# Norm sums folded on VectorE ahead of TensorE's products, and the square moved up ScalarE's step

## The reference, cut to what matters

```
for i in range(DEPTH):                                  # 6
    x = attn_layer(shift_tokens(x), ...) + x            # the sum is called x1 in the kernel
    x = ffn_layer(shift_tokens(x), g, bln, W1, b1, W2, b2) + x

def ffn_layer(x, g, bln, W1, b1, W2, b2):
    mu = x.mean(-1, keepdims=True)
    var = ((x - mu) ** 2).mean(-1, keepdims=True)
    xn = (x - mu) / jnp.sqrt(var + 1e-05) * g + bln
    ...
```

## Time and profile before

| | |
|---|---|
| median of 3 runs | 3278.15 us (3271.11 to 3278.32) |
| profiled execution: span from first to last instruction | 3280.4 us |
| its own time beside the span | the page gives none apart from the span, which lies 2.2 us above the median of the runs |
| TensorE matmul busy | 3087.2 us, 94% |
| TensorE weight load busy | 2736.1 us, 83% |
| VectorE busy | 2638.4 us, 80% |
| ScalarE busy | 2534.1 us, 77% |
| GpSimd busy | 2084.0 us, 64% |
| mean granted TensorE clock | 0.963 |

### The profile page before, as it was taken

The page is one execution under the profiler, slowest core; times in us unless marked ns, Lnnn a source line. Parts: engine busy times, 40 slices in busy tenths (PEclk is TensorE's granted clock), DMA queues, the critical chain, the costliest instruction groups (busy, mean ns, idle before and its releaser), DMA issues. The chain is left out here.

```text
span 3280.4 us, 80720 instructions
## 1 busy us (share of the span) xinstructions
PE 3087.2 (94%) x29936; PEld 2736.1 (83%) x29936; DVE 2638.4 (80%) x5117; ACT 2534.1 (77%) x7059; POOL 2084.0 (64%) x1536
## 2 busy tenths in 40 slices
PE   5898886689999999999999999999999999999997
PEld 4666664479998999989999989999899998999996
DVE  3378888878789888788878898878988878888884
ACT  2787885478787888788888888888788887888784
POOL 5347655776666666666666676667676767666661
PEclk8888996799999999999999999999999999999998
DMA  3111100110001000001100011000100000110000
GB/s 128 55 36 49 59 4 7 42 36 11 2 2 34 25 26 2 2 21 33 31 2 2 11 34 39 1 2 2 37 26 22 2 1 21 33 31 7 8 5 26
DMA packets 27780, 75.04 MB, mean 23 GB/s; under 512 B 4120, under 2 KB 9848, under 8 KB 27256
## 3 DMA queue, kind: packets, MB, share of 16 engines
q1 hardware_dynamic: 22224, 52.63, 5.1%
q0 software_dynamic: 4864, 16.78, 1.6%
q10 hardware_dynamic: 304, 0.47, 0.1%
HBM read 65.68 MB, written 4.19 MB: 21 GB/s over the span
## 5 line engine op out<-in xcount | busy, mean ns | idle before, releaser
L1596 POOL TENSOR_TENSOR turned<-by_cos,turned 128x512 f32<-128x512 f32 x384 | 494.5, 1288 | 827.5 <-DVE turned L2101 827.0
L1600 POOL TENSOR_TENSOR rnorm<-norm,half 128x8 f32<-128x8 f32 x384 | 789.1, 2055 | 0.0
L1883 ACT ACTIVATE prob<-ps_s,ebias,rnorm 128x128 f32<-128x128 f32 x1536 | 681.8, 457 | 64.9 <-DVE ebias L2122 64.2
L2115 DVE TENSOR_REDUCE negmax<-ps_s 128x8 f32<-128x1024 f32 x192 | 235.0, 1224 | 284.0 <-PE ps_s L1698 283.9
L1892 ACT ACTIVATE prob_t<-ps_t 128x512 f32<-128x512 f32 x384 | 230.3, 600 | 223.4 <-PE ps_t L1707 218.8
L2130 DVE TENSOR_TENSOR prob<-prob,rinv 128x512 f32<-128x512 f32 x384 | 375.8, 979 | 13.1
L1642 PE MATMUL ps_qk<-w_hi,x_hi 128*128 128x512 f32 x768 | 336.8, 438 | 18.8 <-DVE turned L2101 12.2
L1787 PE MATMUL ps_f<-hid_hi,w_hi 128*128 128x256 f32 (+1 forms) x1056 | 309.3, 293 | 5.7 <-DVE hid_lo L2176 5.6
L1883 ACT ACTIVATION_READ_ACCUMULATOR prob<-ps_s,ebias,rnorm 128x1 f32 x1536 | 311.1, 203 | 0.0
L1642 PE MATMUL ps_qk<-w_lo,x_hi 128*128 128x512 f32 x768 | 305.8, 398 | 0.0
L1642 PE MATMUL ps_qk<-w_hi,x_lo 128*128 128x512 f32 x768 | 305.7, 398 | 0.0
(11 more groups left out here) (289 smaller groups left out, 9779.6 us busy)
## 6 DMA issues: line engine op xcount, KB each, us to landing
w_raw<-in_w_qkv SPq DMA_DIRECT2D x24, 768.0 KB, 4.8
w_raw<-in_w SPq DMA_DIRECT2D x12, 693.0 KB, 4.0
w_raw<-in_w_o SPq DMA_DIRECT2D x12, 512.0 KB, 3.4
w_raw<-in_w SPq DMA_DIRECT2D x6, 768.0 KB, 4.4
x_tok<-in_x SPq DMA_DIRECT2D x8, 256.0 KB, 2.7
kept<-x_t SPq DMA_DIRECT2D x8, 256.0 KB, 2.0
w_raw<-kept SPq DMA_DIRECT2D x8, 256.0 KB, 3.1
out<-rows_out SPq DMA_DIRECT2D x8, 256.0 KB, 2.2
```

Source lines behind the costliest of these rows:

```text
L1596: G.tensor_tensor(turned[:, k, :], by_cos[:, :], turned[:, k, :], ALU.add).then_inc(s["turned"], 1)
L1600: G.tensor_tensor(rnorm[:, i % RR, :], norm2[:, k, :], half[:, :], ALU.pow).then_inc(s["rnorm"], 1)
L1883: last = A.activation(prob[:, k, h, :], half_bank(h % 2, k)[:, T(h // 2)], ACT.Exp, bias=ebias[:, i // NU % 2, k, h:h + 1], scale=rnorm[:, ...
L2115: V.tensor_reduce(negmax[:, k, :, :].rearrange("p u (c o) -> p o u c", o=2), ps_s[:, :, :].rearrange("p o (u c k) -> p o u c k", u=NU, c=2 ...
```

## The change

- `add_x` on VectorE has a second instruction: it waits for the first, and adds the two halves of x1 (in the shifted view) into `halves`, 128x256, which lies in `hidden[:, 2, :]`.
- `mean_mm` is one product (of `halves`) instead of two.
- A new piece `add_squares` on VectorE (offset 18, behind `soften` and ahead of `rotate`) waits for ScalarE's squares and adds their two halves into `squares`, 128x256, which lies in `gate[:, 2, :]`.
- `var_mm` has two products instead of four, and waits for `add_squares`.
- `square` on ScalarE stands ahead of `project` in step 17 instead of behind `flip_prob`. Its waits are the same, its wait for `hid_lo` too.
- The semaphores `lx1` and `cent` become `x1_and_halves` and `cent_and_squares`, which count two steps for each pass.

```diff
+    halves, squares = hidden[:, KT, :], gate[:, KT, :]
...
         def mean_mm(q):
-            E.wait_ge(s["lx1"], q + 1)
+            E.wait_ge(s["x1_and_halves"], 2 * q + 2)
...
-            for kt in range(KT):
-                last = E.matmul(ps_f[1][:, 0:N], mean_w[:, :], shifted(x1[:, q % 2, :])[:, kt, :], start=kt == 0, stop=kt == KT - 1)
-            last.then_inc(s["mean"], 1)
+            E.matmul(ps_f[1][:, 0:N], mean_w[:, :], halves, start=True, stop=True).then_inc(s["mean"], 1)

         def var_mm(q):
-            E.wait_ge(s["cent2"], q + 1)
+            E.wait_ge(s["cent_and_squares"], 2 * q + 2)
             for u in range(NU):
-                for kt in range(KT):
-                    last = E.matmul(ps_f[1][:, N + u:N + u + 1], cent_sq[:, kt, T(u)], mean_w[:, 0:1], start=kt == 0,
-                                    stop=kt == KT - 1)
+                last = E.matmul(ps_f[1][:, N + u:N + u + 1], squares[:, T(u)], mean_w[:, 0:1], start=True, stop=True)
             last.then_inc(s["var"], 1)
...
         def square(q):
-            A.wait_ge(s["cent"], q + 1)
+            A.wait_ge(s["cent_and_squares"], 2 * q + 1)
             if q:
                 A.wait_ge(s["hid_lo"], 2 * q)
...
+            for q in passes(t, 17):
+                square(q)
             for i in units(t, 0):
                 project(i)
...
-            for q in passes(t, 17):
-                square(q)
             for c in lates(t, 13):
                 flip_heads(c)
...
         def add_x(q):
...
-                            ALU.add).then_inc(s["lx1"], 1)
+                            ALU.add).then_inc(s["x1_and_halves"], 1)
+            V.wait_ge(s["x1_and_halves"], 2 * q + 1)
+            if q:
+                V.wait_ge(s["gated"], 2 * q - 1)
+            by_half = shifted(x1[:, q % 2, :])
+            V.tensor_tensor(halves, by_half[:, 0, :], by_half[:, 1, :], ALU.add).then_inc(s["x1_and_halves"], 1)
...
+        def add_squares(q):
+            V.wait_ge(s["cent2"], q + 1)
+            V.tensor_tensor(squares, cent_sq[:, 0, :], cent_sq[:, 1, :], ALU.add).then_inc(s["cent_and_squares"], 1)
...
             for r in groups(t, 4):
                 soften(r)
+            for q in passes(t, 18):
+                add_squares(q)
             for i in units(t, 1):
                 rotate(i)
```

More of the change, by code:

```diff
@@ L1420 @@
     "qk_square v_copied qk_t prob prob_t attn_hi cent2 lin_hi hid_read_act gelu hid_hi "
-    "qk_by_sin norm2 norm2_floor negmax ebias rinv prob_unit attn_lo lx1 cent spread normed lin lin_lo hid_read_dve gated "
+    "qk_by_sin norm2 norm2_floor negmax ebias rinv prob_unit attn_lo x1_and_halves cent_and_squares spread normed lin lin_lo hid_read_dve gated "
     "fed summed rnorm turned k_unit rstd hid_lo lset"
@@ L1793, in w_2_mm @@
                 E.wait_ge(s["low"], OTHER * (q // B + 1))
-            E.wait_ge(s["lx1"], min(q + 2, PASSES))
+            E.wait_ge(s["x1_and_halves"], 2 * min(q + 2, PASSES) - 1)
             for j in range(NJ):
@@ L2152, in center @@
             V.tensor_tensor(cent[:, :, :], shifted(x1[:, q % 2, :]), ps_f[1][:, 0:N].unsqueeze(1).broadcast_to([P, KT, N]),
-                            ALU.subtract).then_inc(s["cent"], 1)
+                            ALU.subtract).then_inc(s["cent_and_squares"], 1)
+        def add_squares(q):
+            V.wait_ge(s["cent2"], q + 1)
+            V.tensor_tensor(squares, cent_sq[:, 0, :], cent_sq[:, 1, :], ALU.add).then_inc(s["cent_and_squares"], 1)
         def take_spread(q):
```

## The result

| | before | after |
|---|---|---|
| median of the runs | 3275.65 us (4 runs, 3271.11 to 3278.32) | 3306.63 us (4 runs, 3304.18 to 3310.97) |
| ratio, 95% interval | | 1.0102 (1.0084 to 1.0119) |
| profiled execution: own time, span | -, 3280.4 us | 3310.97 us, 3309.7 us |
| TensorE busy, mean granted clock | 3087.2 us, 0.963 | 3057.8 us, 0.962 |

The change costs 1.0%, some 31 us. The forecast was 3305 us, with a range of 3290 to 3322, and a rise of 26.8 us. TensorE is busy 29 us less and the span is 29 us longer: the removed products are gone, and more than their time has come back as waiting.

What follows compares the result with a forecast made beforehand. TensorE is busy 94%, but its waits for other engines decide. 10.5 + 7.0 + 4.6 + 5.1 - 0.4 = +26.8 us gives a span of 3307 us, a median of 3305 us, range 3290 to 3322.

Steps and rivals of the forecast that it cites:

- mean_mm, gain 0: TensorE, border of steps 16 and 17: 0.44 us saved is lost in flip_qk's wait for prob_t; gain 0.
- ordinary passes: The 30 passes without weight splits: new stall of 0.75 us less var_mm's 0.40, 0.35 us longer each, +10.5 us.
- var_mm, 0.40: TensorE: four fewer records, no wait right behind, so 0.40 us gained per pass, 18.8 us over 47.
- halves, 0.47: VectorE, second instruction of add_x: pieces behind it 0.47 us later, rotate and GpSimd's chain 0.17 us late.
- kind 22: Passes like 22, five with weight splits, VectorE without a gap: +1.8 us less 0.40, 1.4 each, +7.0 us.
- The square's place, the main term: ScalarE, ahead of project: square's wait for hid_lo holds the queue, making flip_qk of step 18 stall 0.75 us.
- The chain: From the end of hid_lo through square, squares of q and k, copies and prob_t to flip_qk: 2.44 us.
- Weight-split passes: The 15 passes like 22, 23 and 24, in which weights are split: +7.0, +4.6 and +5.1 us.
- kind 23: Passes like 23, five; hid_lo's lateness set by a weight split: +1.3 us less 0.4 each, +4.6 us.
- kind 24: Passes like 24, five with weight splits: flip_qk +1.4 us, less 0.4 each, +5.1 us.
- No third cost there: Later in step 18: ScalarE catches up, rotate 0.5 us later, but GpSimd had waited 2.40 us; no further cost.
- The port of VectorE and GpSimd: Exclusion rule for both new VectorE additions against GpSimd's SBUF reads; left out of the forecast, sum otherwise 3324, chance 0.12.

Runs made afterwards that it cites:

- The mean's half alone: Kernel before with only `halves` added on VectorE and one product in mean_mm; square and var_mm as before: 3278.08 us, ratio 1.0008.
- `prob_t` out of the way: Kernel before with ScalarE's copy prob_t made between v_tok and v_shift in the step of mean_mm: 3266.08 us, ratio 0.9971.
- The loosened wait: Changed kernel, but the square waits only for the first part of hid_lo (2q - 1), not both: 3266.99 us, ratio 0.9976 to the kernel before.
- the move alone: Kernel before with nothing but the square moved ahead of project: 3325.73 us, ratio 1.0157.
- the old place: Changed kernel with the square back behind flip_prob, its wait unchanged: 3287.14 us, ratio 1.0034 to the kernel before.
- a second addition: Changed kernel with the wait for hid_lo loosened to its first part and add_squares done twice: 3288.08 us, ratio 1.0038 to the kernel before.

## Why the prediction was right, point by point

- **mean_mm, gain 0: shown.** The mean's half alone changes ordinary passes by 0.00 to 0.03 us, and with `prob_t` out of the way the same place gives 0.37.
- **var_mm, 0.40: shown.** In step 18, from `flip_qk` to `flip_prob`, the kernel after takes 3.02 us and the kernel before 3.43: 0.41.
- **halves, 0.47 for the pieces behind it, 0.17 through to GpSimd, and 0.47 ahead of kind 22: shown.** L2127 starts 1.27 us behind `add_x` (0.79 before): 0.48. `hid_lo` ends 7.51 us behind the transposes of step 16 instead of 7.36: 0.15. Ahead of kind 22: 0.45.
- **The square's place, the main term: shown.** The loosened wait removes it with everything else in place, and the move alone brings it about. The square's waits in the list are 105.1 us, a little above the 80 to 100 foretold. The chain measures 2.37 us (1806.22 to 1808.59) for 2.44; the link taken at 0.33 was 0.27. With that the stall is 0.65 us instead of 0.75, and an ordinary pass +0.24 instead of +0.35. (The bounds were carried over inexactly: 0.5 and 1.1 us less 0.40 are 0.1 and 0.7, not 0.14 and 0.75. That moves the range by 1 or 2 us.)
- **Weight-split passes: mechanism shown, sizes near.** Kind 22 came out at 1.0 to 1.45 in the pass plus 0.5 ahead of it (1.4 forecast for both), kind 23 at 0.6 to 0.8 (0.95 forecast), kind 24 at 0.9 to 1.2 (1.05).
- **Not forecast: the clock.** Two episodes in passes 6 and 30 cost some 2.8 us each above the others of their kind. Between 5 and 6 of the 31 us are theirs.
- **The total: in part luck.** The rise was forecast at 26.8 us and is 31.0. That 3305 lies within 2 us of 3306.63 comes also from the median before, which a fourth run lowered by 2.5 us. And the terms of the 26.8 missed in both directions: some 2.5 us too much in the ordinary passes, 1 too much in kind 23, 1.6 too little in and ahead of kind 22 even without the clock, and nothing for the clock (5.6 us) and for the end (3.4 us in the profile). The mechanism and the places are right; the closeness of the number is not evidence for it.
- **"No third cost there": right for this kernel only.** The late `rotate` did no harm because TensorE was late too. Where the stall is cured it comes out: the old place gives +0.34% instead of the -0.35% that I had expected, and a second addition is paid in full. The step that failed is the one on what is late next: it weighed `rotate` against GpSimd and its results in step 19, and not against `project` of step 18, which waits for it by `qk_by_sin`. The list of waits before, 1000 to 3200 us, had a row on this very wait, from the passes of kind 22, which the prediction left out:

```profile
PE ps_qk L1642 <- DVE turned L2101: 0.9, 5, 0.2
```

- **The port of VectorE and GpSimd.** The Trainium skill's rule (SBUF — State Buffer, § Who interferes with whom) that two SBUF inputs of a VectorE instruction block GpSimd's reads would have made GpSimd's chain longer by up to 0.41 us. It did not strike: `hid_lo` moved by 0.15, which VectorE's lateness explains, and GpSimd's L1604 in pass 20 takes 0.61 us at 1803.84. GpSimd was idle when `add_squares` ran, so that addition tests nothing. `halves` ran from 1797.23 in 0.43 us, while GpSimd's power function (L1601, from 1797.13, 1.65 us, its inputs in SBUF) was already under way; by the rule `halves` should have waited for it, and it did not. So beside this instruction the rule does not come out, and the measurement decides; beside L1603 in pass 22 it did (2.14 us).

## What to carry to other kernels

A piece that is moved up in an in-order queue takes its waits along; look up when each of its semaphores is signalled, and what stands behind it that used to stand in front. A wait that hardly showed in the old place (10.9 us in 40 passes) may be stricter than it needs to be: here one of two parts was enough, and that one token is worth some 40 us. And work removed from an engine that is 99% busy is worth nothing if the next instruction waits for another engine, as behind `mean_mm`; the gain lies in that wait (0.3% for moving one copy by 0.4 us), so remove it first.

## What the runs showed of the hardware

Short waits of TensorE can cost more than their length, through the clock. In the kernel with the move alone TensorE waits 1.0 to 1.3 us for `prob_t` in step 18 of each of the 15 passes of weight splits (and in kind 22 another 1.3 us for `hid_lo` just ahead). In 9 of them the granted clock then went to its lower level, and each such pass cost 1.6 to 1.9 us more than most of those with the same waits at the upper level (in kind 22 that is a single pass). The changed kernel has waits of 1.1 to 1.4 us in the same places, and the lower level in 2 of the 15 passes; there it lasted about twice as long as in a pass of the move alone, and cost 2.8 us each. In the traces of the other eight kernels `flip_qk` does not wait in step 18 (in two of them `project` waits up to 0.55 us there), and the clock stayed at its upper level in all passes from 1 to 45, though each has the 1.3 us for `hid_lo` in kind 22. All this rests on one trace of each kernel. Why the same waits lead to it in one pass and not in the next of the same kind is left open: no experiment here shifts them on purpose.
